# Three inverse roots finished on GpSimd, VectorE's work reordered at both borders of an attention loop, and the context loaded first in each step

## What is computed

```python
x = x + tanh(g_xattn[0]) * xattn(layernorm(x), ctx)      # 32 batches of 128 x 128, 16 heads of 64
x = x + tanh(g_ffn[0])   * ffn(layernorm(x))

# layernorm(x) = (x - mean) / sqrt(var + 1e-5)
# xattn: q = x@Wq, k = ctx@Wk, v = ctx@Wv per head; softmax(q k^T / 8) v; @Wo + bo
# ffn:   scores = sigmoid(x@gate_w^T); best 2 of 4 groups, best 8 experts of them;
#        sum over experts of weight * down(silu(gate(x)) * up(x)), plus one shared expert
```

## Time and profile before

| | us |
|---|---|
| median of 3 runs | 658.36 (658.17 to 658.58) |
| the profiled execution | 658.34 |
| its span | 656.6 |
| PE busy | 640.5 (98%) |
| DVE busy | 543.3 (83%) |
| ACT busy | 390.2 (59%) |
| POOL busy | 334.5 (51%) |

### The profile page before, as it was taken

How to read it: one execution, slowest core, us unless ns; L and a number is a source line. 1 busy time by engine, 2 the same in 40 slices (tenths; PEclk the granted TensorE clock), 3 DMA queues, 4 the chain that set the end, 5 groups by cost and what they waited for, 6 DMA issues and landing times.

```text
span 656.6 us, 14063 instructions
## 1 busy us (share of the span) xinstructions
PE 640.5 (98%) x3765; PEld 483.2 (74%) x3765; DVE 543.3 (83%) x1380; ACT 390.2 (59%) x739; POOL 334.5 (51%) x364
## 2 busy tenths in 40 slices
PE   8998999999999999999999999999999999999998
PEld 6656766777667777677557878788887878888786
DVE  7988889989998998999877969878695977869565
ACT  4565656666676666766565455655555555555644
POOL 4223454564444654446302656566575656656563
PEclk9999999999999999999999999999999999999999
DMA  6323232223223323222225744272635436364550
GB/s 183 104 66 82 64 82 64 81 75 83 81 65 84 85 67 91 79 69 81 54 66 152 176 107 128 76 164 80 165 113 121 126 79 149 85 160 113 131 146 17
DMA packets 58429, 65.60 MB, mean 100 GB/s; under 512 B 26256, under 2 KB 35344, under 8 KB 58384
## 3 DMA queue, kind: packets, MB, share of 16 engines
q1 hardware_dynamic: 58384, 65.07, 38.5%
HBM read 61.64 MB, written 2.88 MB: 98 GB/s over the span
## 4 chain that ended last, share of the span: by engine, by line
PE 83%; DVE 4%; DMA 3%; issue 3%; ACT 2%; SPq 1%; DVEq 0%; POOL 0%; ACTq 0%; POOLq 0%
PE bank L1270 17%; PE bank L1271 16%; PE bank L1272 16%; PE bank L1370 8%; PE bank L1394 7%; PE bank L1317 4%; PE bank L1337 3%; PE bank L1346 2%; PE bank L1340 2%; PE bank L1343 2%; PE bank L1357 2%; DVE halves L867 2%; PE bank L1358 1%; PE bank L1360 1%; ACT halves L580 1%
## 5 line engine op out<-in xcount | busy, mean ns | idle before, releaser
L554 POOL TENSOR_TENSOR halves<-area,halves 128x512 fp32r<-128x512 f32 x134 | 174.2, 1300 | 140.3 <-ACT halves L711 135.3
L732 ACT ACTIVATE area<-bank 128x512 f32<-128x512 f32 x136 | 81.4, 598 | 111.2 <-PE bank L1272 110.1
L1226 DVE TENSOR_TENSOR bank<-area,bank 128x512 f32<-128x512 f32 x128 | 88.5, 691 | 50.9 <-PE bank L1272 50.5
L649 ACT ACTIVATE area<-bank 128x512 f32<-128x512 f32 x128 | 69.5, 595 | 102.3 <-PE bank L1346 102.3
L1270 PE MATMUL bank<-x2t_hi,w_hi 128*128 128x512 f32 x272 | 110.3, 405 | 0.1
L1271 PE MATMUL bank<-x2t_hi,w_lo 128*128 128x512 f32 x272 | 107.1, 394 | 0.0
L1272 PE MATMUL bank<-x2t_lo,w_hi 128*128 128x512 f32 x272 | 106.3, 391 | 0.0
L489 POOL TENSOR_TENSOR ctx_hi<-ctx_raw,ones_col 128x128 fp32r<-128x128 f32 x32 | 21.2, 662 | 145.5 <-DMA ctx_raw<-ctx_t 145.5
L711 ACT ACTIVATE halves<-area 128x512 fp32r<-128x512 f32 x136 | 85.1, 626 | 16.9 <-DVE area L1237 15.7
L1237 DVE TENSOR_TENSOR area<-bank,wbc 128x512 f32<-128x512 f32 x128 | 86.1, 677 | 1.4 <-DMA wbc<-rows_dram 1.4
L876 DVE TENSOR_REDUCE row_max<-bank 128x4 f32<-128x512 f32 x128 | 81.9, 682 | 2.2 <-DVE mean_var L777 0.7
(11 more groups left out here) (154 smaller groups left out, 1267.4 us busy)
## 6 DMA issues: line engine op xcount, KB each, us to landing
wbc<-rows_dram SPq DMA_DIRECT2D x126, 256.0 KB, 4.3
inverse_bc<-inverse_dram SPq DMA_DIRECT2D x64, 256.0 KB, 3.6
w_raw<-experts SPq DMA_DIRECT2D x32, 102.0 KB, 2.0
x_sb<-x SPq DMA_DIRECT2D x8, 256.0 KB, 3.3
ctx_raw<-ctx_t SPq DMA_DIRECT2D x32, 64.0 KB, 1.9
ctx_keys<-ctx_nat SPq DMA_DIRECT2D x32, 64.0 KB, 2.0
out<-area SPq DMA_DIRECT2D x7, 256.0 KB, 3.9
max_rows<-max_t SPq DMA_DIRECT2D x64, 4.0 KB
```

What stands on the lines that cost most here:

```text
L554: nc.gpsimd.tensor_tensor(hid_lo[:, u % SLOTS, :], hid[:, u % HIDS, :], raw(hid_hi[:, u % SLOTS, :]), ALU.subtract).then_inc(hidlo_ready, 1)
L649: nc.scalar.activation(probs_t[:, k, :, :], st_ps[q][:].rearrange("p (h n) -> p h n", h=4), ACT.Exp)\
L732: nc.scalar.activation(silu_g[:, u % 2, :], gate_ps[u % 2][:], ACT.Silu).then_inc(silu_ready, 1)
L1226: nc.vector.tensor_tensor(up_ps[u % UPS][:], silu_g[:, u % 2, :], up_ps[u % UPS][:], ALU.mult)\
```

## The change

It has four parts.

1. Three of the five roots (n = 1, n = 2, and the first 24 tiles' second one) keep their first four instructions on VectorE; the Newton steps go to GpSimd, where the fused third instruction of a step becomes two (four a step, twelve in all). `rstd_level` now takes the engine.
2. VectorE's order in chunk 0 and chunk 7: `STATS_AT`, the first residual and the root's head come earlier, `normalise` stands ahead of `ln2_apply` in chunk 7's first step and the root's head ahead of its maxima; two levels of routing move from the last half-step to the one before (`SEAM`).
3. SyncE's step begins with the context load.
4. `max_scores` of tile 2 waits for the maxima of one half only.

```diff
-LN_AT = {0: range(0, 8), 1: range(8, RSTD_LEVELS)}
-STATS_AT = {2: (2,), 3: (3,), 4: (4,), 5: (5,), 6: (6, 7)}
+STATS_AT = {2: (2,), 3: (3, 4), 4: (5,), 5: (6,), 6: (7,)}
-SEAM = {4: (1, 6), 5: (6, 10), 6: (10, 14), 7: (14, 21)}
+SEAM = {4: (1, 6), 5: (6, 10), 6: (10, 16), 7: (16, 21)}
...
+        def rstd_level(seq, eng, which, n, batches, level):
...
+                elif eng is nc.vector:
+                    ins = eng.scalar_tensor_tensor(guesses[i + 1], product, 1.5, guesses[i], ALU.add, ALU.mult)
+                else:
+                    eng.tensor_scalar(product, product, 1.5, None, ALU.add).then_inc(newton_step, 1)
+                    seq.wait_ge(newton_step, NEWTON_STEPS * (n - 1 if which == 0 else AHEAD) + i + 1)
+                    ins = eng.tensor_tensor(guesses[i + 1], product, guesses[i], ALU.mult)
...
 # SyncE, attention
+                    if not last:
+                        wait_first(ctx_ready, t + 1)
+                        load_raw(b, (t + CB) * P)
                     if not (last and b == CB - 1):
                         load_max_row(t + 1, (b + 1) % 2, t - 1)
                     if not (first and b == 0):
                         spread_sums(t - 1, (b - 1) % CB)
-                    if not last:
-                        wait_first(ctx_ready, t + 1)
-                        load_raw(b, (t + CB) * P)
...
 # GpSimd
+            def inverse_root(which, n, batches):
+                for level in range(GUESS_LEVELS, RSTD_LEVELS):
+                    rstd_level(pool, nc.gpsimd, which, n, batches, level)
+
             def attention(c, first, last):
+                if last:
+                    inverse_root(1, 0, slice(0, NB_SEAM))
                 for b in range(CB):
...
+                if first:
+                    inverse_root(0, 2, slice(2 * CB, NB))
+            inverse_root(0, 1, slice(CB, 2 * CB))
...
 # VectorE, attention of the first and last chunk
+                        if last and step_of_chunk == 0:
+                            for level in range(GUESS_LEVELS):
+                                rstd_level(dve, nc.vector, 1, 0, slice(0, NB_SEAM), level)
                         if not (last and b >= 2):
                             for q in range(2):
                                 take_max(t + 2, b % 2, h, q)
                         if h == 0 and not first:
                             batch_stats(t - CB, b)
+                        if first and step_of_chunk == 3:
+                            chunk_stats(STATS_AT[3][0])
+                        if first and step_of_chunk == 7:
+                            for level in range(GUESS_LEVELS):
+                                rstd_level(dve, nc.vector, 0, 2, slice(2 * CB, NB), level)
+                            residual(0)
                         if h == 1 and b % 2 == 1 and first:
                             g_low(2 * c + 2 + b // 2, b // 2)
...
-                            if not (first and b < 3):
+                            if not first:
                                 residual(t - 3)
...
-                            if step_of_chunk == 0:
-                                for level in range(RSTD_LEVELS):
-                                    rstd_level(1, 0, slice(0, NB_SEAM), level)
-                                ln2_apply(0, 0)
...
                         if h == 0 and not first:
                             normalise(t - 2, (b - 2) % CB, 0)
+                        if last and step_of_chunk == 0:
+                            ln2_apply(0, 0)
...
 # TensorE, max_scores
-                    wait(pe, max_ready, 4 * t + 2 * h)
+                    wait(pe, max_ready, 4 * t - 2 if h == 0 and isinstance(t, int) and t == 2 else 4 * t + 2 * h)
```

More of the change, by code:

```diff
@@ L54 @@
 NEWTON_STEPS = 3
-RSTD_LEVELS = 3 + 3 * NEWTON_STEPS
+GUESS_LEVELS = 3
+RSTD_LEVELS = GUESS_LEVELS + 3 * NEWTON_STEPS
 RSTD_STEPS = RSTD_LEVELS + 1
@@ L281, in steps_before @@
             return ROUTE_STEPS * c + (1 if c > 0 else 0)
+        def rstd_level(seq, eng, which, n, batches, level):
+            width = batches.stop - batches.start
+            scratch = ln_small if width <= 2 * CB else ln_large
+            v, w, bits, first_guess, odd_guess, even_guess, square, product = (
+                scratch[:, k, 0:width] for k in range(8))
+            variance, base, stepped = mean_var[:, which, batches, 1], RSTD_STEPS * n, rstd_step[which]
+            i, newton_op = divmod(level - 3, 3)
+            if level == 0:
+                if which:
+                    seq.wait_ge(means_kept, batches.stop // CB)
+                else:
+                    seq.wait_ge(ln_step[0], 2 * batches.stop)
+                eng.tensor_scalar(v, variance, EPS, None, ALU.add).then_inc(stepped, 1)
+                eng.tensor_scalar(w, variance, EPS, -0.5, ALU.add, ALU.mult).then_inc(stepped, 1)
+            elif level == 1:
+                seq.wait_ge(stepped, base + 2)
+                eng.tensor_scalar(bits.bitcast(I32), v.bitcast(I32), 1, 0x7fffffff,
+                                        ALU.logical_shift_right, ALU.bitwise_xor).then_inc(stepped, 1)
+            elif level == 2:
+                seq.wait_ge(stepped, base + 3)
+                eng.tensor_scalar(first_guess, bits, GUESS_SCALE, None, ALU.mult).then_inc(stepped, 1)
+            else:
+                guesses = (first_guess, odd_guess, even_guess, rstd[:, which, batches])
+                seq.wait_ge(stepped, base + level + 1)
+                if newton_op == 0:
+                    ins = eng.tensor_tensor(square, guesses[i], guesses[i], ALU.mult)
+                elif newton_op == 1:
+                    ins = eng.tensor_tensor(product, square, w, ALU.mult)
+                elif eng is nc.vector:
+                    ins = eng.scalar_tensor_tensor(guesses[i + 1], product, 1.5, guesses[i], ALU.add, ALU.mult)
+                else:
+                    eng.tensor_scalar(product, product, 1.5, None, ALU.add).then_inc(newton_step, 1)
+                    seq.wait_ge(newton_step, NEWTON_STEPS * (n - 1 if which == 0 else AHEAD) + i + 1)
+                    ins = eng.tensor_tensor(guesses[i + 1], product, guesses[i], ALU.mult)
+                ins.then_inc(stepped, 1)
         block = stack.enter_context(nc.Block())
@@ L1062, in _ @@
             for level in range(RSTD_LEVELS):
-                rstd_level(0, 0, slice(0, CB), level)
+                rstd_level(dve, nc.vector, 0, 0, slice(0, CB), level)
             dve.wait_ge(rstd_step[0], RSTD_STEPS)
@@ L1124, in attention @@
                         if first:
-                            for level in LN_AT.get(step_of_chunk, ()):
-                                rstd_level(0, 1, slice(CB, 2 * CB), level)
+                            if step_of_chunk == 0:
+                                for level in range(GUESS_LEVELS):
+                                    rstd_level(dve, nc.vector, 0, 1, slice(CB, 2 * CB), level)
                         if last:
-                            if step_of_chunk == 0:
-                                for level in range(RSTD_LEVELS):
-                                    rstd_level(1, 0, slice(0, NB_SEAM), level)
-                                ln2_apply(0, 0)
                             if step_of_chunk == 4:
@@ L1141, in attention @@
                             route_levels[0](0, ut_ps)
-                        if first and step_of_chunk == 7:
-                            for level in range(RSTD_LEVELS):
-                                rstd_level(0, 2, slice(2 * CB, NB), level)
             def steady_attention(c):
```

37 lines of the change are left out of this document (4 added, 33 removed).

## The result

The changed kernel takes 662.18 us (median of 6, 661.55 to 663.72) and the kernel before 658.22 us (6 runs) beside it: ratio 1.0069, 95% interval 1.0054 to 1.0084. The forecast was 658.5 us, with a range up to 661.4 us. The profiled execution took 662.33 us and has a span of 660.5 us.

A forecast was written before the change was run, and what follows sets the result against it. TensorE was taken to bound the kernel (83% of the chain), with some 8 us to win at the borders. From 658.34 us, -1.6 + 2.65 - 1.06 + 0.2 = +0.2 us gave 658.5 us, range 654.7 to 661.4 us.

The forecast's parts named there:

- First border: Start of the attention: VectorE's new work order and moved roots were to save time, -1.6 us, bounds -2.6 and -0.6.
- (b): First border: one chunk's statistics leave the place ahead of tile 5's second reduction, so a 0.76 us wait goes.
- (c): First border: the first residual moves ahead of four subtractions and two normalises, so the transpose's 1.58 us wait goes.
- (a): First border: tile 2's maxima product no longer waits for both halves of tile 1, gaining 0.3 us, at most 0.76.
- 1.8 us of VectorE's lateness was the root: First border, reciprocal at 69.46 us: the root on VectorE was said to cause 1.8 us of its lateness.
- Context first: Loop: the context load ahead of row maxima and sums adds 0.61 us at each tile; +2.65 us in all.
- The first pass, +0.65: Loop's first pass: the second tile's slack is used up, so the early context load costs 0.65 us there.
- Last border, routing: End of the attention: two routing steps move one step earlier, so the weight is ready sooner and TensorE saves 1.06 us.
- Last root: Last border: the root's Newton steps on GpSimd make VectorE's layernorm wait; +0.2 us, ends -0.3 and +0.6.
- the load is free: Rival, loop: slack in SyncE's queue hides the early context load, which costs nothing; 654.9 us, chance 0.27.
- GpSimd is slow at small work: Rival, roots: GpSimd needs 0.6 us an instruction, 7.2 us a root, so layernorms wait; 663.5 us, chance 0.06.
- The ring takes more: Rival, fourth tile of each loop pass: SyncE's queue costs 0.85 us a pass; 661.3 us, chance 0.17.

## Why the prediction was wrong

The measured time lies above the whole range. Three terms failed: the price of the load in the loop and that of the last root were too small, and the clock was in no term.

- **First border, -1.6 us.** The working was right in direction and short in size: 2.4 us at the same scores. (b) and (c) hold, as both gaps went; (a) gave 0.6 us, of which 0.1 us was left by 51.7 us. What failed is "1.8 us of VectorE's lateness was the root": with the root back on VectorE the reciprocal still waits 1.00 us for its sums, and the gain is the same (0.9929 against 0.9945, overlapping intervals). The order alone frees the reciprocal. I had also left out the wait of 1.04 us before the output projection at 95.04 us: it follows a normalise whose reciprocal waited 2.06 us for its sums, and it is gone, so TensorE is 3.8 us ahead at the scores behind it (93.64 us, 97.49 us before). Without the load this lead stays, 3.1 to 3.9 us in three profiles.
- **Context first, +0.61 us a step.** The mechanism is right and shown by three runs: behind, by another queue, doubled. The size is not. The fourth tile costs 0.45 us a pass against my 0.4. The first tile, which I had not priced, costs 0.2 us: its reciprocal waits 1.07 us for the sums (0.34 us at 192.83 us before), and the output projection starts as soon as the normalise behind it ends, at 194.43 + 2.90 = 197.33 us:

```profile
193.89 0.25 DVE L907 RECIPROCAL inverse<-sums 128x16 f32<-128x16 f32 x1 [1.07 <-DMA sums<-u_odd]
...
194.43 2.90 DVE L913 TENSOR_TENSOR area<-area,inverse_bc 64x1024 f32<-64x1024 f32 x2
```

```profile
197.43 2.02 PE L1415 MATMUL bank<-c_pair,area 128*128 128x128 f32 x16
```

  So a pass costs 0.7 us in the result's profile and in that of the changed kernel taken again, and 0.7 to 0.95 us on average in those of the other kernels with one load ahead. Five passes cost 3.4 to 4.7 us and not 2.0. The first pass, +0.65, costs 0.7 us in one execution and 1.6 us in another: its wait of 1.44 us is 0.55 us in the first of them. Why executions differ so is open.
- **Last border, routing, -1.06 us.** Right, by the rows; too small to show in the time.
- **Last root, +0.2 us.** This term failed as a mechanism. I had VectorE wait 1.0 us for GpSimd's root; it waits 2.10 us, which is the sign of being wrong that I had named. One instruction of the twelve is held up (1.23 us instead of 0.23), which I had priced at 0.9 us and then given a small weight. The Trainium skill's lock (SBUF — State Buffer, SBUF: two separate sides) speaks of the whole instruction, and the rows agree: 1.23 us beside a normalise of 1.22 us, 1.18 us in another run. What I had not seen is the other direction: the layernorm, 1.1 us in the earlier trace rows, takes 2.12 us beside GpSimd's split of the weights, which stands right behind the root in GpSimd's list and so starts at the same moment. Holding GpSimd gives 1.12 us and takes 1.1 us off the gap. TensorE loses 1.1 us at this border without a fall, over my upper end of 0.6, and 2.2 to 2.5 us in the profiles with one. With the root on VectorE it loses nothing, and the ratio is 1.0017 against 1.0045 and 1.0069 for the changed kernel.
- **The clock.** No step and no rival had it. In the series of the result each execution had one or two falls. Without a fall the changed kernel takes 659.9 us, 2.1 us over the kernel before without one; my sum had 0.2. So about half of the miss is the mis-sized terms, and the rest is what goes with the falls. One execution without a fall took 658.95 us, near my 658.5; that is the lowest of seventeen and no support for the sum.
- The rival "the load is free" falls, as does "GpSimd is slow at small work" (0.23 us an instruction; I took 0.24). "The ring takes more" had the right place, and its 0.85 us a pass lies within the 0.7 to 0.95 us of the profiles. It also comes nearest in time, 661.3 us, but that is partly luck: it had neither the last border nor the clock.

## What to carry to other kernels

Price a transfer that is moved ahead of others in one queue as an issue in every round trip that passes through that queue, at each tile and not only where the slack is smallest, and try it on a queue outside the ring. Before moving small work to GpSimd, look at what GpSimd does the moment it is done as well as at what VectorE does meanwhile. When an edit makes a gap longer in a TensorE-bound kernel, count a possible fall of the clock beside the gap itself (0.5 to 2.5 us between the medians here), and compare executions with the same mean clock.

## What the hardware showed unexpectedly

- The granted clock falls to 0.50 for some 3.4 us behind gaps of TensorE of 1.44, 2.03 and 2.58 us, but not each time: gaps of 1.52 and 2.54 us were passed at 1.00, and one fall came behind a gap of 0.76 us. What decides it stays open. Executions of one kernel with one fall have medians 0.5 to 2.5 us above those with none.
- VectorE's 128x24 instructions take 0.18 us, and up to 0.52 us beside GpSimd's splits; GpSimd's take 0.23 us, and up to 1.23 us beside a normalise. A tensor_scalar with one large input (the layernorm) is slowed too, from 1.11 to 2.12 us for four. The Trainium skill's rule for the lock (SBUF — State Buffer, SBUF: two separate sides) names VectorE instructions with two SBUF inputs or in a mode with two ports; no run here tells which of the two this one is.
- A load issued by GpSimd takes 0.57 us of GpSimd, and a pass of the loop is as long with it as in the kernel before, 40.4 us.
